# A new first stage for an attention and mixture-of-experts block: strips of q and k first, a second head group of direct products, splits on GpSimd

## The reference

```python
mod = (_silu(L0_c) @ L0_wmod).reshape(L0_c.shape[0], 6, 1, -1)
sa, ca, ga, sb, cb, gb = ...
ga = (2 * (ga >= 0) - 1) * jnp.maximum(jnp.abs(ga), 0.25)      # gb the same
h = _layernorm(x) * (1 + ca) + sa
x = x + ga * attention(h)      # 16 heads of 8 channels; Wq, Wk, Wv, Wp made alpha * sign(W)
h = _layernorm(x) * (1 + cb) + sb
x = x + gb * ffn(h)            # a shared expert and 2 of 8 routed ones, 256 wide
# attention, for each batch and head:
q, k, v = split_heads(_binlinear(h, W, b))
att = softmax(einsum('bhtd,bhsd->bhts', q, k) * Dh ** -0.5)
y = einsum('bhts,bhsd->bhtd', att, v)
```

## Time and profile before

| | |
|---|---|
| three runs, us | 667.86, 669.41, 663.66 (median 667.86) |
| the profiled execution | 667.02 us, its span 665.2 us, mean granted clock 0.977 |
| TensorE busy | 615.2 us (92% of the span) |
| VectorE busy | 504.9 us (76%) |
| ScalarE busy | 404.1 us (61%) |
| GpSimd busy | 259.2 us (39%) |
| first scores of batch 0 | 37.40 us |

### The profile page before, as it was taken

One profiled execution on the slowest core, in us unless ns is written; L12 is line 12 of the kernel. 1 busy time (PEld: TensorE's weight loads), 2 busy tenths in 40 slices (PEclk: granted clock), 3 DMA queues, 4 the chain that ended last, 5 costly groups with the idle time before them and its releaser, 6 DMA issues.

```text
span 665.2 us, 10688 instructions
## 1 busy us (share of the span) xinstructions
PE 615.2 (92%) x3461; PEld 288.7 (43%) x3461; DVE 504.9 (76%) x1065; ACT 404.1 (61%) x791; POOL 259.2 (39%) x309
## 2 busy tenths in 40 slices
PE   4899999999999999999999999999999589886997
PEld 2332324233333333423333333232378578776855
DVE  5779788889988989888998888988467534433567
ACT  2345777777777776777778778678735224433431
POOL 4240041414352451434336235025056656566610
PEclk9969999999999999999999999999999988997999
DMA  3443332442541445344244244214832223222155
GB/s 103 134 121 117 117 114 98 132 131 90 160 123 64 133 134 134 109 149 116 93 147 127 69 133 130 67 50 135 226 81 57 68 65 88 63 68 61 56 185 195
DMA packets 58828, 73.91 MB, mean 111 GB/s; under 512 B 10857, under 2 KB 39819, under 8 KB 58772
## 3 DMA queue, kind: packets, MB, share of 16 engines
q1 hardware_dynamic: 53144, 63.30, 32.0%
q0 software_dynamic: 4320, 8.47, 3.7%
q10 hardware_dynamic: 1308, 1.46, 0.8%
HBM read 38.36 MB, written 34.96 MB: 110 GB/s over the span
## 4 chain that ended last, share of the span: by engine, by line
PE 73%; DVE 12%; ACT 7%; issue 3%; another core or an unknown queue 2%; DMA 1%; SPq 1%; POOL 1%; ACTq 1%; DVEq 0%; POOLq 0%
PE pv L1620 15%; PE st L1609 15%; PE mx L1594 14%; PE mx L1806 7%; DVE neg_max L1077 6%; PE st L1820 5%; PE mx L1754 3%; PE misc L1487 2%; PE misc L1514 2%; PE st L1770 2%; ACT pt L868 2%; PE pv L1794 1%; PE misc L1520 1%; DVE stats_sb L1026 1%
## 5 line engine op out<-in xcount | busy, mean ns | idle before, releaser
L868 ACT ACTIVATE pt<-st 128x512 f32<-128x512 f32 x496 | 282.1, 598 | 105.8 <-PE st L1609 95.9
L1077 DVE TENSOR_REDUCE neg_max<-mx 128x2 f32<-128x1024 f32 x248 | 294.5, 1215 | 47.9 <-PE mx L1594 44.6
L1620 PE MATMUL pv<-pt,vs 128*32 128x512 f32 x1024 | 136.4, 605 | 0.3 <-ACT pt L868 0.3
L745 POOL DMA_INDIRECT routed<-rec,row_u x64 | 64.1, 1002 | 136.6 <-PE pv L1620 114.8
L812 POOL DMA_INDIRECT results<-qs,home_u x71 | 72.0, 1014 | 50.8 <-ACT qs L995 28.4
L1609 PE MATMUL st<-even_qk 74*128 74x512 bf16 x256 | 89.0, 389 | 1.9 <-ACT pt L868 1.1
L1609 PE MATMUL st<-qs,ks 74*128 74x512 bf16 x240 | 81.4, 383 | 1.8 <-ACT pt L868 1.1
L1594 PE MATMUL mx<-ks,qs 72*128 72x512 bf16 x256 | 76.5, 380 | 2.9 <-DVE neg_max L1077 2.5
L1594 PE MATMUL mx<-even_qk 72*128 72x512 bf16 x240 | 74.5, 393 | 4.4 <-DVE neg_max L1077 4.1
L437 POOL TENSOR_TENSOR qk_r<-qk_f,qk_parts 128x512 f32<-128x512 f32 x15 | 17.4, 1161 | 98.8 <-DVE qk_parts L429 98.7
L1609 PEld LDWEIGHTS st<-even_qk 74*128 74x128 bf16 x256 | 20.9, 99 | 71.5 <-ACT pt L868 51.7
(11 more groups left out here) (217 smaller groups left out, 798.0 us busy)
## 6 DMA issues: line engine op xcount, KB each, us to landing
routed<-pad_rows SPq DMA_DIRECT2D x64, 260.0 KB
even_qk<-q_parts SPq DMA_DIRECT2D x48, 96.0 KB
qs<-q_parts SPq DMA_DIRECT2D x48, 96.0 KB
ks<-k_parts SPq DMA_DIRECT2D x48, 96.0 KB
even_qk<-k_parts SPq DMA_DIRECT2D x42, 96.0 KB
ks<-routed SPq DMA_DIRECT2D x28, 130.0 KB
q_parts<-qk_parts SPq DMA_DIRECT2D x21, 128.0 KB
k_parts<-qk_parts SPq DMA_DIRECT2D x7, 384.0 KB, 2.3
```

The lines of the kernel that those rows point to most:

```text
L745: pool.indirect_dma_start(out=routed_dram, out_offset=bass.IndirectOffsetOnAxis(ap=row_u[:, k, t:t + 1], axis=0), in_=rec[b.par][:, k, t, ...
L868: act.activation(pt[n % 2][:, hh, :], score_bank(b, n, hh), ACT.Exp, scale=SCALE).then_inc(exp_done, 1)
L1077: dve.tensor_reduce(neg_max[g % 2][:, hh, 2 * half:2 * half + 2], mx_bank[half][:], AX_X, ALU.max, negate=True).then_inc(mx_free, 1)
L1620: last = pe.matmul(pv_bank[32 * hh:32 * (hh + 1), :], vs[b.par][:, j, HG * g + hh, :], pt[n % 2][:, hh, :], start=(n % Y_SLOTS == 0), stop ...
```

## The change

DIRECT becomes 2, and DIRECT_FILLS 12: fills 8 to 11 (heads 4 and 5) are made as direct products too, from strips of the second head group, which are projected after fill 5; fills 12 to 15 come from the stack as before. TensorE makes the strips of k and q ahead of the projections of q and k. The bias products wait for bq and bk alone, under a semaphore of their own. The transpose and the split of group 0's maxima come directly after fill 7, ahead of batch 1's ln1, q and k, and VectorE normalises batch 1 after them. GpSimd makes both splits of batch 0 and 1 / sigma of batch 1 ahead of its later constants. On SyncE x of batch 1 moves ahead of five small loads, x of batch 2 behind stack 1, and the waits ahead of stacks 2 and 3 go; stack 1 of k moves from ScalarE's queue to SyncE's. ScalarE loads the ones later and evacuates v ahead of k's stores.

```diff
-DIRECT = 1
-DIRECT_FILLS = DIRECT * 2 * HG
+DIRECT = 2
+DIRECT_FILLS = 3 * HG
...
-        BEFORE = ["c", "mod", "ln1_0", "q_0", "k_0", "v_0", "ln1_1", "q_1", "m0", "k_1"]
+        BEFORE = ["c", "mod", "ln1_0", "q_0", "k_0", "v_0", "m0", "ln1_1", "q_1", "k_1"]
...
# SyncE
-            for i, w in enumerate((Wq, Wk, Wv, Wp)):
-                sp.dma_start(w_nat[:, i, :], w).then_inc(w_loaded[i // 2], 16)
-            for i, v in enumerate((bq, bk, bv)):
-                sp.dma_start(bias_qkv[:, i:i + 1], v.rearrange("(p o) -> p o", o=1)).then_inc(small_loaded, 16)
+            for i, w in enumerate((Wq, Wk)):
+                sp.dma_start(w_nat[:, i, :], w).then_inc(w_loaded[0], 16)
+            for i, v in enumerate((bq, bk)):
+                sp.dma_start(bias_qkv[:, i:i + 1], v.rearrange("(p o) -> p o", o=1)).then_inc(qk_bias_loaded, 16)
+            for i, w in enumerate((Wv, Wp)):
+                sp.dma_start(w_nat[:, 2 + i, :], w).then_inc(w_loaded[1], 16)
...
+            load_x(B1)
+            sp.dma_start(bias_qkv[:, 2:3], bv.rearrange("(p o) -> p o", o=1)).then_inc(small_loaded, 16)
...
-            load_x(B1)
             sp.wait_ge(parts_ready, 1)
             store_q_heads(0, HG, first_stored[0])
             store_q_heads(HG, H, q_stored)
-            load_x(B1.plus(1))
             sp.wait_ge(first_stored[0], 16 * PARTS)
             load_q_stack(B0, 0)
-            load_q_stack(B0, 1)
-            sp.wait_ge(stack_loaded[0][1], STACK_DMAS)
-            sp.wait_ge(m_row_loaded[0], ROW_DMAS)
-            for g in (2, 3):
+            for g in (1, 2, 3):
                 load_stack(B0, g)
+                if g == 1:
+                    load_x(B1.plus(1))
...
# GpSimd, behind 1 / sigma of batch 0
+            split_qk(pool, B0, 0)
+            split_qk(pool, B0, 1)
+            rstd(mv1, ve1, var1_ready, rstd1, rstd1_ready, stats1_ready, B1)
             pool.affine_select(out=earlier_token[:], ...
...
             pool.wait_ge(setup_pool, 4)
-            rstd(mv1, ve1, var1_ready, rstd1, rstd1_ready, stats1_ready, B1)
-            split_qk(pool, B0, 1)
             fill_values(pool, 1)
...
# ScalarE
-            act.wait_ge(setup_pool, 3)
-            for i in range(2):
-                load_ones(act, i)
...
             evacuate_wT(0, 2)
-            act.wait_ge(small_loaded, 80)
-            evacuate_qk(B0, 0, use(AHEAD, "q_0"))
             act.wait_ge(first_done, 1)
             evacuate_direct(1, 0, 3)
             evacuate_direct(0, 0, 4)
+            evacuate_qk(B0, 0, use(AHEAD, "q_0"))
             evacuate_qk(B0, 1, use(AHEAD, "k_0"))
+            act.wait_ge(setup_pool, 3)
+            load_ones(act, 0)
             evacuate_wT(2, 5)
             act.activation(exp_first[:], strip_rows[:], ACT.Exp)
+            act.wait_ge(v_ready[0], 2)
+            evacuate_v(B0, use(AHEAD, "v_0"))
             act.wait_ge(parts_ready, 2)
             for h0, h1, stored in ((0, HG, first_stored[1]), (HG, H, k_stored)):
                 act.dma_start(k_dram[0][h0:h1].rearrange("h d i t -> (h d) i t"), qk_parts[1][DH * h0:DH * h1]).then_inc(stored, 16)
-            act.wait_ge(v_ready[0], 2)
-            evacuate_v(B0, use(AHEAD, "v_0"))
+            evacuate_direct(1, 1, 6)
+            evacuate_direct(0, 1, 7)
             act.wait_ge(key_ones[0], 16)
             load_k_stack(act, B0, 0)
-            load_k_stack(act, B0, 1)
-            project_in(B1, use(AHEAD, "ln1_1"))
-            evacuate_qk(B1, 0, use(AHEAD, "q_1"))
+            act.wait_ge(small_loaded, 48)
             act.wait_ge(misc_free, use(AHEAD, "m0") + 1)
             for k in range(M_PARTS):
                 act.dma_start(qs[0][MROW + k:MROW + k + 1, 0:HG, :]...
+            project_in(B1, use(AHEAD, "ln1_1"))
+            evacuate_qk(B1, 0, use(AHEAD, "q_1"))
+            load_ones(act, 1)
             evacuate_qk(B1, 1, use(AHEAD, "k_1"))
...
# VectorE
             first_part(dve, B0, 0, use(AHEAD, "q_0"))
-            split_qk(dve, B0, 0)
+            maxima(range(1))
+            first_part(dve, B0, 1, use(AHEAD, "k_0"))
+
+            maxima(range(1, 2 * HG))
+            split_max(B0, 0, use(AHEAD, "m0"))
             layer_norm1(B1)
-            first_part(dve, B0, 1, use(AHEAD, "k_0"))
-
-            maxima(range(DIRECT_FILLS))
-            split_max(B0, 0, use(AHEAD, "m0"))
-            maxima(range(DIRECT_FILLS, FIRST_FILLS))
+            maxima(range(2 * HG, FIRST_FILLS))
...
# TensorE
-                        pe.wait_ge(first_done, (4,)[g])
+                        pe.wait_ge(first_done, (4, 7)[g])
...
-                if hh == 0 and half == 0:
+                if hh == 0 and half == 0 or fill == DIRECT_FILLS:
                     pe.wait_ge(stack_loaded[b.par][g], STACK_DMAS * (b.half + 1))
...
-                pe.wait_ge(small_loaded, 80)
+                pe.wait_ge(qk_bias_loaded, 32)
...
-            pe.wait_ge(first_done, 2)
+            free(use(AHEAD, "q_0"))
+            project_direct(1, 0, 2)
+            project_direct(0, 0, 2)
             project(0, use(AHEAD, "q_0"))
-            project_direct(1, 0, 1)
-            project_direct(0, 0, 2)
             project(1, use(AHEAD, "k_0"))
...
                 if fill == 5:
+                    project_direct(1, 1, 4)
+                    project_direct(0, 1, 4)
+                if fill == 2 * HG - 1:
+                    max_T(B0, 0, use(AHEAD, "m0"))
+                if fill == 2 * HG:
                     ln1_T(B1, use(AHEAD, "ln1_1"))
-                if fill == DIRECT_FILLS - 1:
+                if fill == 2 * HG + 1:
                     project(0, use(AHEAD, "q_1"))
-                    max_T(B0, 0, use(AHEAD, "m0"))
             project(1, use(AHEAD, "k_1"))
```

More of the change, by code:

```diff
@@ L215, in adaln_block @@
         small_loaded = sem("small_loaded")
+        qk_bias_loaded = sem("qk_bias_loaded")
         c_loaded = sem("c_loaded")
@@ L694, in _ @@
             rstd(mv1, ve1, var1_ready, rstd1, rstd1_ready, stats1_ready, B0)
-            pool.affine_select(out=earlier_token[:], in_=ones_bf[:], compare_op=ALU.is_gt, fill=0.0, base=0,
-                               pattern=[[1, P]], channel_multiplier=-1).then_inc(consts_ready, 1)
-            pool.memset(marks[:], 0.0).then_inc(consts_ready, 1)
-            pool.sem_inc(rows_free, 2)
-            pool.iota(expert_no[:], pattern=[[1, E]], base=0, channel_multiplier=0,
-                      allow_small_or_imprecise_dtypes=True).then_inc(consts_ready, 1)
-            pool.iota(next_row[0][:], pattern=[[REGION, E]], base=0, channel_multiplier=0,
-                      allow_small_or_imprecise_dtypes=True).then_inc(consts_ready, 1)
-            for k in range(RING):
-                pool.memset(digit[:, k:k + 1], float(E ** k)).then_inc(consts_ready, 1)
-            pool.memset(pad_rows[:], 0.0).then_inc(pad_ready, 1)
-            pool.wait_ge(pad_ready, 1)
-            pool.memset(pad_rows[:, :, C + 1], float(FAR)).then_inc(pad_ready, 1)
-            pool.iota(first_row[:], pattern=[[REGION, E]], base=0, channel_multiplier=0,
-                      allow_small_or_imprecise_dtypes=True).then_inc(consts_ready, 1)
-            pool.iota(unit_start[:], pattern=[[P, 2 * EARLY_PAIRS]], base=0, channel_multiplier=0,
-                      allow_small_or_imprecise_dtypes=True).then_inc(consts_ready, 1)
-            pool.affine_select(out=earlier[:], in_=ones_bf[:, 0:E * E].rearrange("p (e f) -> p e f", e=E), compare_op=ALU.is_gt,
-                               fill=0.0, base=0, pattern=[[1, E], [-1, E]], channel_multiplier=0).then_inc(consts_ready, 1)
-            pool.iota(home[:], pattern=[[TOKENS, K_TOP], [1, TT]], base=0, channel_multiplier=TT,
-                      allow_small_or_imprecise_dtypes=True).then_inc(setup_pool, 1)
             def residual(b):
```

27 lines of the change are left out of this document (24 added, 3 removed).

## The result

The changed kernel takes 677.43 us (median of 4 runs, 671.73 to 678.04), the kernel before in the same session 667.29: a ratio of 1.0157, 95% interval 1.0114 to 1.0199. The forecast was 667.7 us, within a range of 663.7 to 671.0: the change is slower, by more than the range allows. The profiled execution took 677.45 us, its span 675.7 (665.2 before).

A forecast was written before the change was run, and what follows sets the result against it. VectorE bounds the catch-up, TensorE the untouched part from about 64 us. Fill 11's maximum at 41.65 instead of 39.35, less 1.59 us of idle time, gives +0.7: 667.02 + 0.7 = 667.7 us, range 663.7 to 671.0.

The forecast's parts named there:

- the middle line: Fills 8 to 11: clock at half until about 38 us, then full, so fill 11's maximum starts at 41.65; forecast chance 0.42.
- The wait of 1.59 us in the catch-up: VectorE's idle time at 45.10 us, with TensorE at half clock; at full clock it goes, saving 1.59 us.
- the catch-up: Stretch from 39.35 to 63.91 us where VectorE takes three maxima a slot and is the bound; same work asked as before.
- What bounds the kernel, and where to look: TensorE sets the pace from about 64 us, untouched; the change is worth what it moves fill 11's maximum, before at 39.35.
- The head: Up to the first direct product: TensorE's first product with hT at about 10.9 instead of 11.83, fill 0 0.65 us earlier.
- The eight fills: Head group 0, VectorE the bound: gaps of 0.8 and 1.4 us, fill 7's maximum ends at 31.2 instead of 30.23.
- Row maxima, GpSimd, the queues: Ahead of the first scores: m_rows ready 1.0 us earlier, later stores and loads costed at nothing; smallest cover 0.9 us.
- the second group's gain: Fill 8: direct products remove its wait for the stack of group 1, at most 0.35 us.
- Fills 8 to 11: Where the new direct products cost: each 1.0 us at full clock, 1.9 at half, against about 0.85 before at half.
- The three lines for fill 11's maximum: Its start by clock: full 39.6, half until about 38 41.65, half throughout 44.55; end moves by -1.3, +0.7 or +3.6 us.
- Rival B: TensorE between 31 and 45 us: clock stays at half through fills 8 to 11, +3.6 us, 670.6; chance 0.22.

The follow-up runs named there:

- a_again: The changed kernel, unaltered, on the later chips: 654.35 us, ratio 1.0246 to the kernel before.
- a_qfirst: The changed kernel with q projected ahead of the strips again: 653.54 us, ratio 1.0195 to the kernel before.
- a_bridge_vsplit: a_bridge with the q split of batch 0 on VectorE instead of GpSimd: 643.49 us, ratio 1.0034 to the kernel before.
- a_onegroup_bridge: The changed kernel with one head group of direct products only, plus spare products ahead of fills 2 to 7 and in the pauses: 643.83 us, ratio 1.0015.
- a_bridge: The changed kernel with spare bf16 products ahead of fills 2 to 7 and in the pauses after fills 7 and 8: 644.15 us, ratio 1.0046.
- c_best: The kernel before with early bias products, moved loads, the maxima's transpose straight after fill 7, and spare products: 639.22 us, ratio 0.9962.
- b_again: The kernel before, unaltered, on the later chips: 639.73 us, ratio 0.9987.
- b_bridge: The kernel before with spare bf16 products in its own pauses: 639.53 us, ratio 0.9990.
- c_best2: c_best with further spare products in fills 9 and 10 and in slot 0: 639.07 us, ratio 0.9946 to the kernel before.
- a_height: The changed kernel with two more f32 products in the idle row groups beside direct fills 0 to 3 and 8 to 10: 642.77 us, ratio 1.0018.

## Why the prediction was wrong

The forecast for the profiled execution was 667.7 us and 677.45 came, 9.75 more. Fill 7's maximum ended 4.7 us later than forecast (35.9 for 31.2). From there to the start of fill 11's maximum it took 14.5 us where the middle line has 10.45, 4.05 more. The wait of 1.59 us in the catch-up that was to go stayed (1.79 at 56.34), and the catch-up took 24.75 us where 22.97 follows from the prediction, 1.8 more. Behind it 0.8 was gained.

**What bounds the kernel, and where to look: right for this execution.** TensorE's steady pace is untouched, the catch-up costs the same as before, and the change is worth what it does to fill 11's maximum: +11.05 us there, 10.5 in the span. In a_again the catch-up is slower too (below).

**The head: right in size.** Fill 0 came 1.0 us earlier instead of 0.65, since the rate rose near 15 us (the q product at 13.97 takes 1.66 us, not 2.08), not at 17.4. The text overlooked that q and k now use one bank back to back, so that k waits 0.78 us for q's evacuation; a_qfirst, without this pause, was not clearly faster.

**The eight fills: right on one execution, wrong on the other.** Forecast was an end of fill 7's maximum at 31.2. In a_again it is 30.6. In the first profile it is 35.9 (33.54 + 2.36), because the clock fell at 21.9 among the direct fills, a case that the prediction did not have: every one of its cases began at 31. It is worth 5 us there and comes in some executions only.

**Row maxima, GpSimd, the queues: right.** No first score waited for a DMA, and the q split's place makes no difference (a_bridge_vsplit). One term was mis-sized: I gave the second group's gain as 0.35 us, from the trace of before, though I had put the k loads of group 1 later myself. In the new order it is worth 3.5 us (a_onegroup_bridge). The forecast time does not contain this term, so it is not what made it wrong.

**Fills 8 to 11: the step that failed is "I take the middle".** The three lines for fill 11's maximum were 39.6, 41.65 and 44.55. With the clock full the profile has 39.9 (a_bridge, with spare products in the pauses); with it at half throughout, 45.0 (a_again). Both ends hold within 0.5 us, the second in part by luck: from the end of fill 7's maximum it took 14.4 us where that line has 13.35, and it began 0.6 earlier. The choice between them did not hold: "TensorE works without a pause and mostly on f32 products, as it did from 11.83 to 17.40, where the rate rose after 5.6 us". The products of 11.83 to 17.40 fill all 128 rows of the array; a direct fill uses two of its four row groups. With these fills TensorE stayed at half clock up to fill 11's maximum and beyond: for 30.8 us in a_again, 20.5 in the first profile, 17.1 in a_qfirst. With the other two row groups filled it came back after 6.8, in both profiles that have this. So busy time alone did not decide when the clock came back, as that sentence assumed. Narrow fills are only part of it, though: behind 45.0 us in a_again, and for 17 us in c_best, the clock stayed at half with no direct fill in the stretch, and no run here separates what its products, most of them bf16 of 72 and 74 rows, do to it. The reading of the fall was loose, too: of the two pauses that the prediction names for it, the second (31.4 to 32.16) comes behind the fall at 31.0. The Trainium skill, TensorE: Matmul & The Clock Gate, section "What's actually happening", says that the ratio is set by how busy the array has been recently. By the profile's busy column that would have given the middle line; the windows of a_again, busy for all of 30.8 us at 0.50, do not agree with that reading of it, and the measurement decides.

**Rival B had the mechanism and the place, but was priced too low.** At 670.6 it counted the loss up to fill 11 alone and took off 1.59 us for a wait in the catch-up that would go. In a_again the clock stays at half to 61.7, through the catch-up, whose fill 25 ends 11.2 us later than in b_again where fill 11 is 5.7 later. In the first profile the clock was back at 56.0, and 4.7 us came ahead of fill 7 instead. Two terms were missing, then: the fall among the first fills, and half clock in the catch-up. B had 0.22; with its own price worked through to the end of the catch-up it would have lain outside the range, and should have widened it.

**What stays open.** With the clock held the changed kernel is still 0.3 to 0.5% behind (a_bridge, a_bridge_vsplit), while fill 25 ends only 0.6 and 1.9 us later than in b_again. What lies behind fill 25 differs by up to 3.7 us between single profiles (576.9 to 580.6), without a trend with the length of the stage (576.9 in b_bridge and 579.7 in c_best2, with 58.2 and 57.9 us ahead). Counting maxima narrows the place: from fill 25's to the last maximum all profiles take 395.6 to 396.7 us, behind it those of the later chips take 180.8 (b_bridge) to 184.3 (a_bridge). This is the stretch of the experts, where VectorE's writes to home_u wait for the DMAs of the experts' results for 8.7 us in b_bridge and 12.8 in a_bridge. No run here tells whether that is chance or hangs on the changed start.

## What to carry to other kernels

Where a change puts narrow products (few row groups of TensorE) into a stage, price it at half clock to the end of that stage, not only at the rate of the row that it is read from: a busy column of 100% is no sign that the clock will return. If TensorE waits in short pauses and has a bank to spare, bridge the pauses with products of full height, or fill the idle row groups beside the narrow ones: in the changed kernel the two were worth 10.2 and 11.6 us. Where the clock is lost for a short time only, there is little to win: bridging the kernel before gave nothing clear of noise (b_bridge). And read several runs: groups of times with their mean clocks show an effect that one profile may miss.

## What the runs showed that was not expected

- 30.8 us at 0.50 with TensorE busy for 14.10 of 14.10 and 16.70 of 16.70 us (a_again), and 17 us with bf16 fills and scores, busy for 16.90 (c_best).
- Two more f32 products of 32 rows beside a fill started within 0.02 us of it and did not lengthen it (a_height).
- Spare work made a kernel faster by 10 us; the mean clock was 0.961 to 0.976 without it and 0.999 to 1.0 with it.
- The first chip took 602 us behind the first stage, the other chips 577 to 581, for the same code; nearly all of it arises behind the last maximum (206.7 us against 180.9), where the first chip's clock falls again, for 17.1 us in all from 529.4 us on, and that of b_again not before 636.3. The loss by the change was 10 us there and 14 here.
